# A preln graph layer on one core: the second bias as a product over 128 rows, and the relative tags of node tiles on GpSimd

## What is computed

```python
h = relu(layernorm(x))
msg_input = concatenate([h[src], h[dst]], axis=1)
for t in range(4):
    m = relu(msg_input @ W1[t] + b1[t]) @ W2[t] + b2[t]
    msgs += where(type == t, m, 0)
agg = segment_sum(msgs, dst)
gi, gh = agg @ W_ih.T + b_ih, h @ W_hh.T + b_hh
r, z = sigmoid(i_r + h_r), sigmoid(i_z + h_z)
n = tanh(i_n + r * h_n)
out = x + (1 - z) * n + z * h
```

## Time and profile before

| | us |
|---|---|
| median of 3 runs (1898.24 to 1906.78) | 1900.25 |
| the profiled execution, whole | 1895.2 |
| its span, from the first to the last instruction | 1893.3 |
| PE busy with products | 1688.8 (89%) |
| DVE busy | 1791.1 (95%) |
| ACT busy | 1539.3 (81%) |
| POOL busy | 1130.8 (60%) |
| mean granted PE clock, share of full speed | 0.972 |

### The profile page before, as it was taken

The page is one execution under the profiler, slowest core; times in us unless marked ns, Lnnn a source line. Parts: engine busy times, 40 slices in busy tenths (PEclk is TensorE's granted clock), DMA queues, the critical chain, the costliest instruction groups (busy, mean ns, idle before and its releaser), DMA issues. The chain is left out here.

```text
span 1893.3 us, 44349 instructions
## 1 busy us (share of the span) xinstructions
PE 1688.8 (89%) x10156; PEld 1422.2 (75%) x10156; DVE 1791.1 (95%) x4457; ACT 1539.3 (81%) x3793; POOL 1130.8 (60%) x1788
## 2 busy tenths in 40 slices
PE   0112599999999999999999999999999999999898
PEld 0002488888888888888888888888888888888787
DVE  8999989999999999999999999999999999999887
ACT  0011499999998899999999999999999999998796
POOL 5654677777777565655556565555656556565310
PEclk9995599999999999999999999999999999999999
DMA  2112467777776766777776777777777776779853
GB/s 67 42 34 53 109 178 192 195 193 191 192 190 180 193 185 187 194 189 188 191 190 185 192 191 188 189 193 186 189 194 191 186 195 187 187 192 169 165 140 97
DMA packets 477058, 319.52 MB, mean 169 GB/s; under 512 B 106707, under 2 KB 463139, under 8 KB 476966
## 3 DMA queue, kind: packets, MB, share of 16 engines
q10 hardware_dynamic: 261792, 156.12, 27.5%
q1 hardware_dynamic: 185734, 106.93, 24.2%
q0 software_dynamic: 29440, 55.47, 13.0%
HBM read 211.59 MB, written 106.72 MB: 168 GB/s over the span
## 5 line engine op out<-in xcount | busy, mean ns | idle before, releaser
L570 POOL DMA_INDIRECT e_x<-in_x,rows_now x816 | 795.6, 975 | 277.1 <-issue 271.0
L1127 ACT ACTIVATE e_h<-e_x,shift,rstd 128x128 f32<-128x128 f32 x816 | 356.6, 491 | 116.0 <-DVE shift L993 116.0
L1144 ACT ACTIVATE n_h<-n_x,shift,rstd 128x128 f32<-128x128 f32 x784 | 361.2, 487 | 0.0
L1288 PE MATMUL bank<-n_h_hi,whh_hi 128*128 128x512 f32 x588 | 248.8, 423 | 8.4 <-ACT n_zc L1244 7.9
L1288 PE MATMUL bank<-n_a_hi,wih_hi 128*128 128x512 f32 x588 | 248.8, 423 | 0.0
L1016 DVE TENSOR_SCALAR n_sel<-iota,n_rel 128x256 fp32r<-128x256 f32 x784 | 240.0, 368 | 4.8 <-ACT n_rel L1195 4.8
L1364 PE MATMUL bank<-n_sel,n_win 128*128 128x256 f32 x1568 | 236.0, 293 | 5.8 <-DVE n_sel L1016 5.8
L1290 PE MATMUL bank<-n_a_hi,wih_lo 128*128 128x512 f32 x588 | 232.7, 396 | 0.0
L1289 PE MATMUL bank<-n_h_lo,whh_hi 128*128 128x512 f32 x588 | 232.5, 395 | 0.0
L1290 PE MATMUL bank<-n_h_hi,whh_lo 128*128 128x512 f32 x588 | 231.8, 394 | 0.0
L1289 PE MATMUL bank<-n_a_lo,wih_hi 128*128 128x512 f32 x588 | 231.8, 394 | 0.0
(11 more groups left out here) (170 smaller groups left out, 4208.6 us busy)
## 6 DMA issues: line engine op xcount, KB each, us to landing
n_win<-messages SPq DMA_DIRECT2D x1568, 64.2 KB
messages<-e_msg ACTq DMA_DIRECT2D x204, 257.0 KB, 2.7
n_x<-in_x ACTq DMA_DIRECT2D x195, 256.0 KB
out<-n_out ACTq DMA_DIRECT2D x195, 256.0 KB
e_x<-in_x,rows_now POOLq DMA_INDIRECT x816
rows_now<-lists SPq DMA_DIRECT2D x204, 2.0 KB
lists<-picks,list_rows POOLq DMA_INDIRECT x72
w<-in_W SPq DMA_DIRECT2D x1, 512.0 KB
```

Source lines behind the costliest of these rows:

```text
L570: G.indirect_dma_start(e_x[:, s, 2 * end + t, :], None, x, bass.IndirectOffsetOnAxis(ap=rows_now[:, s, t, end:end + 1], axis=0)).then_inc( ...
L1127: last = A.activation(e_h[:, s % 2, k, :], e_x[:, s, k, :], ACT.Relu, scale=rstd[:, slot, col + k:col + k + 1], bias=shift[:, slot, col + ...
L1144: last = A.activation(n_h[:, s % 2, cols], n_x[:, s, cols], ACT.Relu, scale=rstd[:, slot, col + 4 + k:col + 5 + k], bias=shift[:, slot, co ...
L1288: T.matmul(o, w_hi, v_hi, start=start, stop=False)
```

## The change

1. `b2_rows` gets 128 rows, of which 2 to 127 are zero: its source is broadcast to 128 partitions (SP's DMA, 2 rows before), and the four operations that make it run over 128 partitions. The product at L1389 (and its twin in `general_sums`, a path that these inputs don't take) has all 128 rows of `ones_r` and `b2_rows`.
2. ACT's two activations for `n_rel` go. POOL makes `n_rel` with one addition over 128 x 4, placed in its step between the first two gathers and the last two. With it go the two waits, for the windows (`n_windowed`) and for the `n_sel` two groups back (`n_seled`).

```diff
-        b2_rows = sb("b2_rows", [2, TYPES * D], F32R)
-        row_is = sb("row_is", [2, 2])
+        b2_rows = sb("b2_rows", [P, TYPES * D], F32R)
+        row_is = sb("row_is", [P, 2])
...
-            e_msg[:].rearrange("p r t w -> p (r t w)")[0:2, at * TYPES * D:(at + 1) * TYPES * D] for at in range(4))
+            e_msg[:].rearrange("p r t w -> p (r t w)")[:, at * TYPES * D:(at + 1) * TYPES * D] for at in range(4))
...
-            sp.dma_start(b2_two[:], b2.rearrange("(a t) o -> a (t o)", a=1).to_broadcast([2, TYPES * D])
+            sp.dma_start(b2_two[:], b2.rearrange("(a t) o -> a (t o)", a=1).to_broadcast([P, TYPES * D])
...
-            def gather(q, m):
+            def gather(q, m, ends_):
                 s = m % UNROLL
-                for end in range(2):
+                for end in ends_:
...
+            def relative_tags(g, m):
+                s = m % 4
+                if not within(g, NG):
+                    return
+                if isinstance(g, int) and g == 0:
+                    pool.wait_ge(s_bases, 1)
+                pool.wait_ge(n_windowed[s], uses(g, s, 4, 128))
+                if due(g - 1):
+                    pool.wait_ge(n_seled, g - 1)
+                G.tensor_tensor(n_rel[:, s % 2, :].rearrange("p (h k) -> p h k", h=2),
+                                n_win[:, s, :, TAG].bitcast(F32).rearrange("p (h k) -> p h k", h=2),
+                                base[:, bass.ds(2 * g, 2)].unsqueeze(2).to_broadcast([P, 2, 2]), ALU.add).then_inc(n_reled, 1)
...
                 if within(i, UNITS):
-                    gather(i, m)
+                    gather(i, m, (0,))
+                relative_tags(i - LAG + 1, m - LAG + 1)
+                if within(i, UNITS):
+                    gather(i, m, (1,))
...
-                V.tensor_scalar(row_is[:, 0:1], part[0:2, :], 0.5, None, ALU.is_lt)
-                V.tensor_scalar(row_is[:, 1:2], part[0:2, :], 0.5, None, ALU.is_gt)
+                V.tensor_scalar(row_is[:, 0:1], part[:], 0.0, None, ALU.is_equal)
+                V.tensor_scalar(row_is[:, 1:2], part[:], 1.0, None, ALU.is_equal)
...
             def step(i, m):
-                g, s = i - LAG + 1, (m - LAG + 1) % 4
-                if within(g, NG):
-                    if isinstance(g, int) and g == 0:
-                        act.wait_ge(s_bases, 1)
-                    act.wait_ge(n_windowed[s], uses(g, s, 4, 128))
-                    if due(g - 1):
-                        act.wait_ge(n_seled, g - 1)
-                    for half in range(2):
-                        rows = slice(2 * half, 2 * half + 2)
-                        last = A.activation(n_rel[:, s % 2, rows], n_win[:, s, rows, TAG].bitcast(F32), ACT.Identity,
-                                            bias=base[:, bass.ds(2 * g + half, 1)])
-                    last.then_inc(n_reled, 1)
...
-                    T.matmul(bank[BE1][:, message_part], ones_r[0:2, :], b2_rows[:, first * D:(first + 2) * D],
+                    T.matmul(bank[BE1][:, message_part], ones_r[:], b2_rows[:, first * D:(first + 2) * D],
```

2 lines of the change are left out of this document (1 added, 1 removed).

## The result

| | before | after |
|---|---|---|
| median of the comparison (6 runs each), us | 1901.52 | 1911.92 |
| lowest and highest | 1898.24 to 1906.78 | 1907.33 to 1915.56 |
| ratio after to before, 95% interval | | 1.0051 [1.0028, 1.0073] |
| span of the profiled execution | 1893.3 | 1913.7 |

The change makes the kernel slower, by 0.5%: 10 us, from 5 to 14. The forecast was 1892 us.

What follows compares the result with a forecast made beforehand. In the loop PE looked like the bound, DVE close behind, with the selection ring capping gains. Terms -12 (loop), +4.5 (tags before it), -1 (end) sum to -8.5 us: 1892 us against the 1900.25 median, 8-in-10 range 1874 to 1911.

Steps and rivals of the forecast that it cites:

- The product's gap: PE around the two-row product L1389: 0.08 lost before and 0.18 behind, so 128 rows save PE 0.26 us a step.
- Rival C: PE at the two-row product: the gap stays, only POOL's cost is left, +4.5, 1905 us; chance 0.08.
- The mean is 0.12 us a step that a faster PE can win: Loop: room before the selection ring binds in all four steps read; 0.09 taken over 134 steps, -12 us.
- one ring, through the selection: Loop: DVE's n_sel releases PE's sum, then ACT's n_a_hi to n_n, then DVE's n_d to next n_sel; caps gain at 0.12.
- ACT's saving 0: ACT behind n_n: without its two tags it only waits longer at n_a_hi, already 0.33 idle, so nothing ends earlier: 0.
- POOL's tag in the loop 0: Loop: POOL idles 1.5 us a step at its gate and the tag is in time for n_sel, so cost 0.
- 45 x 0.10 = +4.5 us: Steps before the loop: POOL has no idle for others, each tag adds its price; ends +1 and +13.
- rival D: Before the loop: tags lock into phase with DVE's n_e and n_xh, 0.6 each, +14, 1914 us; chance 0.16.
- has to fall back once: DVE before the loop: the late tag sets its n_sel back once, then steps 20 to 63 go at POOL's pace.
- The end -1: After step 198: edge units run out and other waits rule; -1 us.
- A: Loop: PE's saving comes through whole as the ring shortens too, -31, 1869 us; chance 0.06.
- B: Before the loop: POOL swallows the tags, the 0.09 holds in all 179 steps, 1883 us; chance 0.22.

Runs made afterwards that it cites:

- e4_order: Kernel before with the 128-row product, tags on ACT, and PE's candidate products ahead of its reset-gate products: 1887.07 us, ratio 0.9915.
- e7_order_loop_tags: Kernel before with the 128-row product, PE's candidate products ahead of its reset-gate products, and tags on POOL only inside the loop: 1890.46 us, ratio 0.9917.
- e14_act_shadow: Changed kernel with two tag-sized spare operations back on ACT before the loop, with the old waits, output unused: 1911.18 us.
- e15_act_ops_only: Changed kernel with two tag-sized spare operations back on ACT before the loop, without the old waits: 1908.83 us.
- e3_loop_only: Changed kernel with tags on POOL only in the loop, on ACT before and after it: 1897.17 us, ratio 0.9969 to the kernel before.
- e1_bias: Kernel before with the 128-row product alone, tags still on ACT: 1894.78 us, ratio 0.9952.
- e8_tag_twice: Changed kernel with POOL's tag made twice before the loop, once into a spare tile: 1920.02 us, ratio 1.0085 to the kernel before.
- e16_act_tied: Changed kernel, before the loop two spare ACT operations with old waits, and DVE's selection waits for them too: 1901.27 us, ratio 0.9992 to the kernel before.

## Why the prediction was wrong

**The product's gap** held: 0.24 and 0.12 where 0.24 and 0.13 were foretold, and 0.28 us a step gone where 0.26 was. The trace is in line with the Trainium skill's TensorEngine Tiling (Array Packing), Key Properties, on the drain at a switch of the tiling mode, but no run here shows that two rows are another mode. By the Trainium skill's TensorE: Matmul & The Clock Gate, LDWEIGHTS (loading the stationary operand), which gives 32 rows the time of 128, the gap would have stayed; it went. Rival C, the gap that stays, fell with that.

**"The mean is 0.12 us a step that a faster PE can win"** is the step that failed. I had found one ring, through the selection, and let it alone cap the gain. I took -12 us (0.09 a step); in the profiles the changed kernel won 0 in the loop, the product alone 4.4. The runs showed the ring through `n_zc` in its place: PE waits there in all 112 steps counted, and it had only 0.065 us a step of room. I had traced what the sum waits for, and what DVE waits for, but not PE's own waits on buffers it writes. In the kernel before, `n_zc` hardly shows as a wait in the loop, because PE came about 0.06 us later than the hand-over needs. The line was in the timeline all the same. The prediction had named the sign of this failure, a loop step at 8.33 with the gaps gone. e4_order fits the cap of 0.12: once the ring through `n_zc` is eased the sum waits for the selection, and the loop has won 0.07.

**ACT's saving 0**: right in the loop (e7_order_loop_tags), and right before it (e14_act_shadow, e15_act_ops_only: giving the time back moves group 45 by no more than the changed kernel's two profiles differ).

**POOL's tag in the loop 0**: right as to the wait. No wait for the tag ends a selection there, and e3_loop_only has the same loop as e1_bias to 0.01. But the changed kernel's own loop is 0.034 longer than e1_bias's, 4.6 us, through ACT's pause ahead of `e_r`; that is the size of the product's gain, and its cause is open.

**"45 x 0.10 = +4.5 us"** was mis-sized: it measured 0.27 a step, 12 us, near the upper end of 0.3 that I had put there and given too little weight. The operation with its surroundings is 0.15 by POOL's account (0.10 to 0.14 for the second one of e8_tag_twice), so 0.10 was low by a third. The larger miss is the meeting. Its price was in view in the earlier trace rows, and in rival D, for the tag itself. But it is mostly the gathers around the tag that meet DVE's two-input operations, and seldom the tag. That the stage ends with POOL's last list write was right. I also wrote that DVE "has to fall back once" and then go at POOL's pace. It does not fall back and stay; it waits in 16 steps. I put this down to the unequal length of POOL's steps before the loop (9.5, 10.1, 9.8 and 5.4 us from gate to gate in the changed kernel), which no run tests.

**"The end -1"**: the two profiles differ by +7.5, of which the repeats leave about 3.

Of the rivals D came nearest, in mechanism and in sign: slower by a dear tag before the loop. I had put its price at 0.6 against the measured 0.27, and set 13 us of gain against it that did not exist. That it said 1914 and 1912 was measured is luck: two errors cancel. A and B fell: the loop's step did not move, and POOL did not swallow the tags. (In e16_act_tied the stage did take them in at no cost, but that needed a wait which the change does not have.) The sum with the measured terms: 0 in the loop, +10 to +12 before it, +3 at the end, which is 13 to 15, at the upper edge of the 5 to 14 that the timed runs give.

**What stays open.** Why the second wait on DVE keeps the gathers off DVE's two-input operations. It may be the 0.07 us by which it delays the selection, so that the gather behind the tag starts unhindered and the pattern of a whole step settles otherwise. It may be the one early group where it does hold the selection. No run separates these. Open too is ACT's longer pause in the loop of the changed kernel.

## What to carry to other kernels

An engine that looks saturated has a reserve of rings right behind its own work. Before crediting a saving to it, list every wait of that engine, also those that never show as idle, and measure for each how long its releaser had been done: the smallest of these numbers caps the gain. And a cheap operation moved onto a queue that never pauses is not priced by its own length alone: as much again can come from which of its neighbours now meet what on other engines, and one wait elsewhere can take that away. Undo each half of such a change before keeping it; here one half was worth -0.5% and the other +0.8%.
